# Column position terms interleaved four to a row in their bank, and evicted in runs of four words

## The reference

```
attn = einsum('bqc,bkc->bqk', q * scale, k)
rel_h = einsum('bhwc,hkc->bhwk', r_q, Rh)     # query (h, w) against the table row of its own h
rel_w = einsum('bhwc,wkc->bhwk', r_q, Rw)     # query (h, w) against the table row of its own w
attn = attn + rel_h[..., :, None] + rel_w[..., None, :]
out = softmax(attn) @ v
```

## Time and profile before

| | us |
|---|---|
| median of 3 runs | 1005.36 (999.14 to 1011.05) |
| the profiled execution's own time | 1006.65 |
| its span, first to last instruction | 1005.0 |
| mean granted TensorE clock | 0.948 of full |
| PE busy | 893.9 (89%) |
| DVE busy | 476.0 (47%) |
| ACT busy | 461.1 (46%) |
| POOL busy | 180.2 (18%) |

### The profile page before, as it was taken

One profiled execution on the slowest core, in us unless ns is written; L12 is line 12 of the kernel. 1 busy time (PEld: TensorE's weight loads), 2 busy tenths in 40 slices (PEclk: granted clock), 3 DMA queues, 4 the chain that ended last, 5 costly groups with the idle time before them and its releaser, 6 DMA issues.

```text
span 1005.0 us, 14977 instructions
## 1 busy us (share of the span) xinstructions
PE 893.9 (89%) x5408; PEld 710.8 (71%) x5408; DVE 476.0 (47%) x1025; ACT 461.1 (46%) x927; POOL 180.2 (18%) x257
## 2 busy tenths in 40 slices
PE   2878979878888889999889889999999989998998
PEld 1755755666575578767667666897599859885898
DVE  5867676695786744442542564016400551045101
ACT  5776557467557624322532343334324343334423
POOL 3040031022000012331420034003400150004100
PEclk9899979979998999985986999999999999999999
DMA  6010000000000010000000020000000000000000
GB/s 184 1 36 2 1 25 10 0 10 21 0 1 1 2 35 10 22 22 10 21 21 0 1 111 0 1 1 16 0 0 0 16 0 0 0 16 1 1 1 16
DMA packets 12707, 15.44 MB, mean 15 GB/s; under 512 B 5312, under 2 KB 10560, under 8 KB 12544
## 3 DMA queue, kind: packets, MB, share of 16 engines
q1 hardware_dynamic: 10656, 9.46, 3.1%
q0 software_dynamic: 2016, 5.51, 1.9%
HBM read 13.39 MB, written 1.57 MB: 15 GB/s over the span
## 4 chain that ended last, share of the span: by engine, by line
PE 69%; DVE 16%; issue 6%; ACT 6%; DMA 1%; SPq 0%; DVEq 0%; POOL 0%; ACTq 0%; POOLq 0%
PE ps L217 19%; PE ps L1346 12%; PE ps L1274 6%; PE ps L1361 4%; DVE area L269 4%; PE ps L1086 4%; PE ps L1167 3%; PE ps L1009 3%; PE ps L989 2%; DVE nm L604 2%; ACT area L832 2%; PE ps L1216 2%; PE ps L969 2%; PE ps L1214 1%; DVE dstat L702 1%
## 5 line engine op out<-in xcount | busy, mean ns | idle before, releaser
L217 PE MATMUL ps<-xs,ws 128*128 128x512 f32 x460 | 128.0, 426 | 11.6 <-DVE xs L496 7.9
L1346 PE MATMUL ps<-area 128*128 128x192 f32 x768 | 127.4, 326 | 0.0
L1346 PEld LDWEIGHTS ps<-area 128*128 128x128 f32 x768 | 124.8, 190 | 2.0 <-issue 0.5
L832 ACT ACTIVATE area<-ps,nm 112x196 f32<-112x196 f32 (+1 forms) x240 | 85.9, 437 | 82.6 <-DVE nm L604 82.5
L217 PE MATMUL ps<-ws,wx 128*128 128x512 f32 x480 | 116.1, 397 | 1.3 <-DVE ws L723 1.3
L217 PEld LDWEIGHTS ps<-xs,ws 128*128 128x128 f32 x460 | 89.3, 202 | 32.3 <-issue 8.8
L937 ACT ACTIVATE area<-ps,bcol 128x512 f32<-128x512 f32 x96 | 65.8, 689 | 86.6 <-PE ps L217 86.5
L217 PEld LDWEIGHTS ps<-ws,wx 128*128 128x128 f32 x480 | 89.2, 188 | 22.7 <-DVE ws L723 3.0
L734 DVE TENSOR_TENSOR area<-ps,area 128x384 f32<-128x384 f32 x32 | 17.9, 558 | 177.8 <-PE ps L1346 177.8
L604 DVE TENSOR_REDUCE nm<-ps 112x4 f32<-112x784 f32 (+1 forms) x72 | 63.0, 876 | 57.3 <-PE ps L989 44.3
L1086 PE MATMUL ps<-ident,area 112*98 112x112 f32 (+1 forms) x480 | 64.1, 275 | 27.1 <-ACT area L844 15.2
(11 more groups left out here) (161 smaller groups left out, 1437.9 us busy)
## 6 DMA issues: line engine op xcount, KB each, us to landing
stage<-in_wall POOLq DMA_DIRECT2D x42, 128.0 KB, 2.4
area<-in_w2e SPq DMA_DIRECT2D x1, 2304.0 KB, 8.4
out<-xres SPq DMA_DIRECT2D x4, 384.0 KB, 2.6
xres<-in_x SPq DMA_DIRECT2D x1, 1152.0 KB, 7.7
area<-in_wall SPq DMA_DIRECT2D x2, 512.0 KB, 5.8
area<-in_w2a SPq DMA_DIRECT2D x1, 576.0 KB, 3.8
room<-in_rel SPq DMA_DIRECT2D x4, 128.0 KB, 5.2
xres<-in_x SPq DMA_DIRECT2D x1, 384.0 KB, 3.2
```

The costliest lines, as they stand in the source:

```text
L217: last = mm(out_, l, r, start=n == 0, stop=n == len(pairs) - 1)
L832: last = A.activation(pp[0:rows, u % 3, k, 0:keys], ps[0:rows, UH * (u % 2) + k // parts, c0:c0 + keys], ACT.Exp, bias=nm[0:rows, u % 2, k ...
L1346: last = mm(ps[:, 4 + b, s * D:s * D + D], hTd[:, m, b * T + s * P:b * T + s * P + P], w2x[:, e * MC + m, :], start=m == 0, stop=m == MC - 1)
```

## The change

The layout of column terms in the bank becomes (a, y, k): the four columns of a step are interleaved. Each of the column matmuls (16 a stage, 64 in all) now writes its 96 words four words apart, at offset k of each group of four. The copy of column terms reads 384 neighbouring words and writes them in runs of four neighbouring words of `qs` (x = 4q to 4q+3), each run 16 words after the one before. Row terms are laid, computed and copied as before. The number, the engine and the order of all instructions and waits stay the same.

```diff
         def position_terms(copy, cols, q):
-            got = ps[:, REL_BANKS[cols][q], 0:384].rearrange("p (k a x) -> p a k x", k=4, a=2 * G)
+            got = ps[:, REL_BANKS[cols][q], 0:384]
+            got = got.rearrange("p (a y k) -> p a y k", k=4, a=2 * G) if cols else \
+                got.rearrange("p (k a x) -> p a k x", k=4, a=2 * G)
             for r in range(HG):
                 rows = slice(64 * (r % 2) + 32 * cols, 64 * (r % 2) + 32 * cols + 32)
                 to = qs[rows, r // 2 * 2 * G:(r // 2 + 1) * 2 * G].rearrange("p a (y x) -> p a y x", x=W)
-                to = to.rearrange("p a y x -> p a x y") if cols else to
-                last = copy(to[:, :, 4 * q:4 * q + 4, :], got[32 * r:32 * r + 32])
+                to = to[:, :, :, 4 * q:4 * q + 4] if cols else to[:, :, 4 * q:4 * q + 4, :]
+                last = copy(to, got[32 * r:32 * r + 32])
             return last
...
                         for cols in range(2):
                             rows = q4.rearrange("p a (y x) -> p a y x", x=W)
-                            last = mm(ps[:, REL_BANKS[cols][step], 96 * k:96 * k + 96], relt[:, W * cols + at, :],
+                            to = ps[:, REL_BANKS[cols][step], 0:384]
+                            to = to.rearrange("p (a y k) -> p k a y", k=4, a=2 * G)[:, k] if cols else \
+                                to[:, 96 * k:96 * k + 96]
+                            last = mm(to, relt[:, W * cols + at, :],
                                       rows[:, :, :, at] if cols else rows[:, :, at, :], start=True, stop=True)
```

## The result

| | before | changed |
|---|---|---|
| median, us (20 runs each) | 1009.99 (998.39 to 1019.16) | 995.60 (991.94 to 1002.78) |
| profiled execution, its span | 1006.65, 1005.0 | 998.86, 997.1 |
| mean granted clock in it | 0.948 | 0.955 |
| DVE busy, us | 476.0 | 459.3 |
| PE busy, us | 893.9 | 889.9 |

The ratio of the changed kernel to the kernel before is 0.988 (95% interval 0.986 to 0.990): 12 us faster, 10 to 14 by the interval. The time lies inside the predicted range, 2.6 us above the value.

The account below looks back on a forecast made before the run. DVE's 16 column copies were taken to bound each of four heads. Saving 3.4 us a stage, 13.6 in all, with column matmuls and the rest at nothing, took 1006.65 to 993.0 us; range 984 to 1003.

Parts of the forecast that it names:

- What bounds: In each of four heads, first scores and DVE's next work wait for DVE's 16 column copies, 3.15 us behind ACT's.
- The copy: DVE's column copy falls from 0.804 to 0.56 us, 0.576 start to start, priced from the residual add; short runs cost nearly nothing.
- DVE's timetable: First head: DVE's four copy groups end 3.75 us earlier, at 44.22, with 0.2 us turned into a wait for PE.
- Who is late next: In the head ACT becomes last by 0.6 us; first scores come 3.16 us earlier, first maximum 3.16 to 3.79.
- The column matmuls: PE's column matmuls writing four words apart cost nothing, hidden under their strided read of 0.16 us a record.
- Rival 2: Strided writes add to strided reads in PE's position-term steps, 0.44 us a step; 10.5 us gained, 996; chance 0.10.
- Rival 3: Column matmuls writing four words apart take 0.32 us a record for 0.16; 3 us slower in all, 1010; chance 0.05.
- The clock: Half or full clock in the head left undecided; a value between taken, 3.4 us a stage, 13.6 us in all.
- Rival 4: Gained and given back: half-clock stretches, as in the MLP, fall otherwise; about 1000 at its bad end; chance 0.07.
- Rival 1: DVE's copies shrink less, deciding from 0.627 us start to start; at 0.69, 8 us gained, 998; chance 0.12.
- Rival 5: Nothing: the change doesn't alter what DVE's copy costs, 1006 us; chance 0.04.

Follow-up runs that it names:

- run 7: Kernel before, with ten idle matmuls (identity times itself, results unread) in PE's wait for DVE's copies in the head; 1013.10 us median.
- run 2: Interleaved bank layout alone: column matmuls write as in the changed kernel, the copy keeps the old order and 16-word write hops; one time, 1010.43 us.
- run 4: Changed kernel with runs of two words instead of four: matmuls write words two apart, the copy writes runs of two; one time, 995.76 us.
- run 3: Changed kernel with row terms interleaved too: row matmuls write four words apart and ACT reads four words apart; one time, 1001.12 us.
- run 5: Changed kernel again, unaltered; 995.63 us median, ratio 0.988 to the kernel before.
- run 10: Changed kernel with idle matmuls where PE stands for 1 to 2 us, at the stage's end and the pipeline's start; 993.42 us median.
- run 12: Kernel before with idle matmuls in the head's wait, at the pipeline's start and at the stage's end; 1005.36 us, ratio 0.984 to the kernel before.
- run 11: Changed kernel with some ACT work moved to DVE or later, and idle matmuls at stage's end and pipeline's start; 987.74 us median, ratio 0.978.
- run 6: Changed kernel with eight idle matmuls at the stage's end, ahead of PE's wait for the projection; 995.44 us.
- run 8: Changed kernel, two key-group parts moved from ACT to DVE and two border adds moved behind the first maximum; 1005.15 us median, ratio 0.993.
- run 1: Changed copy with the old bank layout: matmuls write neighbouring words, the copy reads with a 96-word hop at every word; one time, 987.24 us.

## Why the prediction was right

- *What bounds*: right. DVE's 16 copies set the scores and the first maximum, in each head; run 7 excludes the clock, run 2 the layout.
- *The copy*: 0.56 taken, 0.554 measured, 0.57 from start to start within a group against 0.576. Taking the price from a residual add of equal size, and the harmlessness of short runs from L589 against L592, held; run 4 shows it for runs of two in the copy itself.
- *DVE's timetable*: groups two to four were to start 2.30, 4.80 and 7.10 us after the first; they started 2.29, 4.80 and 7.09 after, the third behind a wait of 0.25 for PE.
- *Who is late next*: ACT, by 0.64 us (0.6 taken). First scores 12.44 us into the head by the sum, 12.48 measured; first maximum 13.56 at full clock, 13.55 measured.
- *The column matmuls*: nothing, as taken, but for a wrong reason. I had them hidden under their strided read; run 3 shows no price even for matmuls that read in runs. Rivals 2 and 3 fall. The rule cited from the Trainium skill ("PSUM — Partial Sum Buffer", Specifications (TRN2)) does not hold in this form: the 128 fp32 matmuls of run 3, all of 96 columns and writing four words apart, ran at an unchanged pace (4.45 us and 4.51 or 4.52 for two steps, in each of its four heads).
- *The clock*: the mis-sized term. I took 3.4 us a stage as a mean of half and full clock in the head. The head's clock was full, so a head gave 3.8. But half clock did not vanish with it: by the trace's clock record the changed kernel has 24 us of it in the four stages, for 41 before. Of the 41, 16 lay in the heads, under DVE's copies, and most of the rest right behind the first maximum, where PE was busy for 7.67 us of 10; of the 24 none lies in a head, and much of it where PE is busy throughout, at the stage's end (6.70 of 6.70) or some 12 us into a pipeline (3.40 of 3.40). A full clock is worth 3.0 to 5.4 us to the changed kernel (runs 5 and 10) and 0.6 to the kernel before (315.47 against run 12's 314.8), in both cases beyond the price of the idle matmuls. With the clock held the stages differ by 15.3; less 3.0 to 5.4, plus 0.6, that is 10.5 and 12.9, what the two profiles of the changed kernel gained in their stages. The ratio says 12. So 13.6 came near it partly by luck: the head was taken for too little, and the loss inside the stages was not in the sum. I read the earlier trace rows as showing that pauses of 1.3 us leave the clock full. They do not show it: the clock had been at half until 51.2 us and had only just risen, and it took the filling of such pauses, all together, to hold it full in run 10. Rival 4, which I gave 0.07 and placed behind the stages, was at work in small, inside them.
- *Rivals 1 and 5*: fell with the first row after.

That half clock in other places ate a part of the gain is shown by runs 10 and 12 as far as the sum goes. That PE's standing is what lets the clock fall is shown for the filled places taken together: the stages of runs 10, 11 and 12 have 0, 3.4 and 3.4 us at half clock, those of the other eleven profiles 20 to 48. For a single place it is not shown, as in run 6 as much half clock stood elsewhere, and in runs 11 and 12 one filled stage's end fell all the same. Why the places change from execution to execution was not found.

## What to carry to other kernels

When two engines do equal copies in unequal time, compare the direction of their innermost runs: laying a result so that at least two neighbouring words leave together is worth a third of a copy, and either the matmul or the copy may do the hopping on the bank's side. Ahead of the edit, work out at what price the next engine takes over; here ACT took over with 0.64 us in hand, and a price of the copy some per cent off would hardly have shown. And count half-clock time by what PE had to do in it: hidden under a wait it is free (heads of 17.3 us at either clock, run 7), and where PE sets the pace the same microseconds cost.

## What the runs showed of the hardware

- DVE's write of fp32 words 16 apart took 804 ns for 384 words, in runs of two or four 554: 0.65 ns more a word. The Trainium skill, "Vector Engine (DVE) Microarchitecture Reference", section 5.2 (Measured stream behaviour on trn2), gives 1.71 ns a column for an output that hops 4 KiB at every element and 1.054 in pairs, measured on another operation; the trace agrees with the difference, (804 - 554)/384 = 0.65. For an output stepping 24 words the same table has 2.50, and the 16-word step here is far from that.
- Reads out of a bank hopping at every word cost neither engine anything: DVE 554 ns with a hop of 96 words, ACT 471 ns with one of four.
- Matmul writes into a bank two or four words apart cost nothing (runs 3 and 4: two steps in 4.45 us as before), while a moving operand read 16 words apart takes 0.16 us a record for 96 columns against 0.105.
- Idle matmuls in the places where PE stood kept the clock at 1.00 over 300 us (run 10; 0.99 in runs 11 and 12). Behind the stages the same code took 657 us in nine profiles, 650 in four and 671 in that of run 8, with 63, 42 and 97 us at half clock; this alone moves the total by 7 us and more.
- What half clock costs hangs on where it falls. One stretch of 3.4 us some 12 us behind the first maximum went with pipelines of 49.7 us (runs 1, 3, 4, 5 and 6) against 48.1 at full clock; one of 3.4 us 3 us behind it, in the fourth pipeline of runs 6 and 7, left that at 47.07, among the shortest of all.
